# Three GINE layers of a graph network: gather indices kept on the chip, a ring of eight groups, sums kept in PSUM

## What is computed

```python
for l in range(3):
    e = edge_attr @ W_lin[l] + b_lin[l]                 # 32 -> 128 features
    msg = jax.nn.relu(x[src] + e)
    agg = jax.ops.segment_sum(msg, dst, num_segments=n)
    h = x + agg
    h = jax.nn.relu(h @ W1[l] + b1[l]) @ W2[l] + b2[l]
    x = jax.nn.relu(batchnorm(h, gamma[l], beta[l]))    # mean and variance over the nodes
```

## Time and profile before

| | us |
|---|---|
| median of three runs | 4933.01 |
| lowest and highest | 4932.24, 4936.58 |
| span of the profiled execution, first to last instruction | 5756.4 |
| TensorE busy in it, modelled | 4376.5 (76%) |
| VectorE busy | 2580.0 (45%) |
| GpSimd busy | 2560.5 (44%) |
| ScalarE busy | 1654.2 (29%) |
| mean granted clock of TensorE | 0.760 |

### The profile page before, as it was taken

The page is one execution under the profiler, slowest core; times in us unless marked ns, Lnnn a source line. Parts: engine busy times, 40 slices in busy tenths (PEclk is TensorE's granted clock), DMA queues, the critical chain, the costliest instruction groups (busy, mean ns, idle before and its releaser), DMA issues. The chain is left out here.

```text
span 5756.4 us, 93753 instructions
## 1 busy us (share of the span) xinstructions
PE 4376.5 (76%) x20714; PEld 3248.6 (56%) x20715; DVE 2580.0 (45%) x5638; ACT 1654.2 (29%) x3154; POOL 2560.5 (44%) x2647
## 2 busy tenths in 40 slices
PE   2799999566777547677477775677765999999995
PEld 2566666344444336666366664566653666666663
DVE  4677777644444432333222232233224445445444
ACT  1455555333343311111111111111112333333332
POOL 0455555255555335555255552555531333333330
PEclk9999999788888855555555555555557999999997
DMA  1333333122222111112121111121111222222220
GB/s 64 84 91 90 93 92 91 45 55 59 59 61 60 39 45 50 46 49 53 36 50 50 48 50 37 48 51 50 50 31 50 74 75 73 74 75 73 74 70 11
DMA packets 302152, 342.02 MB, mean 59 GB/s; under 512 B 154871, under 2 KB 227396, under 8 KB 301854
## 3 DMA queue, kind: packets, MB, share of 16 engines
q0 software_dynamic: 101632, 237.91, 15.2%
q1 hardware_dynamic: 182910, 79.61, 6.1%
q10 hardware_dynamic: 17568, 24.01, 1.5%
HBM read 324.54 MB, written 15.96 MB: 59 GB/s over the span
## 5 line engine op out<-in xcount | busy, mean ns | idle before, releaser
L777 POOL DMA_INDIRECT gath<-source_rows_narrow,idx x1176 | 1140.4, 970 | 1157.4 <-issue 865.6
L805 PE MATMUL psum<-hot,pm 128*128 128x128 f32 x2928 | 758.3, 441 | 601.6 <-ACT pm L860 566.6
L805 PEld LDWEIGHTS psum<-hot,pm 128*128 128x128 f32 x2928 | 651.4, 327 | 690.0 <-ACT pm L860 591.7
L903 POOL DMA_INDIRECT gath<-source_rows,idx x488 | 462.5, 948 | 879.5 <-issue 716.4
L795 PE MATMUL psum<-gine_lin,ea 32*128 32x128 f32 x2928 | 757.2, 436 | 56.0 <-DMA ea<-in_edge_attr 54.8
L860 ACT ACTIVATE pm<-vs 128x512 f32<-128x512 f32 x366 | 230.3, 629 | 1893.3 <-DVE vs L830 1609.5
L795 PEld LDWEIGHTS psum<-gine_lin,ea 32*128 32x128 f32 x2928 | 650.2, 323 | 141.0 <-DMA ea<-in_edge_attr 79.8
L556 POOL DMA_INDIRECT gath<-source_rows,idx x488 | 473.3, 970 | 556.3 <-PE psum L605 288.8
L556 POOL DMA_INDIRECT gath<-source_rows_narrow,idx x488 | 478.9, 981 | 440.1 <-PE psum L605 171.4
L830 DVE TENSOR_TENSOR vs<-psum,gath 128x512 f32<-128x512 f32 x366 | 253.2, 692 | 666.1 <-remote 292.0
L588 PE MATMUL psum<-lk,att_b 128*128 128x512 f32 x732 | 420.1, 663 | 131.5 <-DVE lk L678 87.9
(11 more groups left out here) (188 smaller groups left out, 5753.6 us busy)
## 6 DMA issues: line engine op xcount, KB each, us to landing
rel<-rel_rows SPq DMA_DIRECT2D x366, 128.0 KB
gath<-source_rows_narrow,idx POOLq DMA_INDIRECT x1664
ea<-in_edge_attr ACTq DMA_DIRECT2D x366, 64.0 KB
gath<-source_rows,idx POOLq DMA_INDIRECT x976
ea<-in_edge_attr SPq DMA_DIRECT2D x122, 64.0 KB
source_rows<-stage SPq DMA_DIRECT2D x12, 512.0 KB, 2.9
idx<-idx_all SPq DMA_DIRECT2D x366, 2.0 KB
source_rows_narrow<-TMP SPq DMA_DIRECT2D x3, 1600.0 KB, 7.3
```

The costliest lines, as they stand in the source:

```text
L777: pool.indirect_dma_start(out=gath[:, slot, j, 0:D], out_offset=None, in_=table1, in_offset=bass.IndirectOffsetOnAxis(ap=idx[:, slot, j:j ...
L805: last = e.matmul(O[s], pm[:, s, j * P:(j + 1) * P], hot[:, s, j, :], start=(j == 0), stop=(j == SUBS - 1))
L903: pool.indirect_dma_start(out=gath[:, s4, j, :], out_offset=None, in_=table, in_offset=bass.IndirectOffsetOnAxis(ap=idx[:, s4, j:j + 1], a ...
```

## The change

The indices of all groups are loaded once, in setup, into `idx_group`; the indirect DMAs read them from there and SP loads none in a layer. The ring has eight slots; `gath` is the same memory, cut into 8 x 4 x 128 in place of 4 x 4 x 256 of which half the width was used. SP only counts freed slots (`gi_free`). The edge features are loaded three items ahead, into four buffers. E has one bank, number 7, and TensorE waits for VectorE's add before it writes the next E. The sums of all blocks stay in banks 0 to 6: TensorE clears them by seven matmuls with zeros, then adds each item's four products at the block's place, whose number it reads into a register; VectorE has no add of the sums, and `gine_mlp` reads them from PSUM. The loops over layers, items and groups are written out.

```diff
+RING = 8
+        idx_group = sb("idx_group", [P, GROUPS, SUBS], I32)
...
+                        sp.dma_start(idx_group[:, :, :], t["src_by_group"]).then_inc(loads, 16)
...
-                        sp.wait_ge(loads, 7 * 16)
+                        sp.wait_ge(loads, 8 * 16)
...
-                        step(v.tensor_scalar(gb_i[:, 1:2], gb_i[:, 0:1], 3, None, ALU.bitwise_and))
+                        step(v.tensor_scalar(gb_i[:, 1:2], gb_i[:, 0:1], RING - 1, None, ALU.bitwise_and))
...
-            E = [psum[:, s, :] for s in range(2)]
-            O = [psum[:, 2 + s, 0:P] for s in range(2)]
+            ring = gath[:, :, :, :].rearrange("p s j d -> p (s j d)").rearrange("p (s j d) -> p s j d", s=RING, d=D)
+            ea_slots = [ea[:, 0, :], ea[:, 1, :], sm[0:EDGE_D, 0, :], sm[0:EDGE_D, 1, :]]
+            flat_psum = psum[:, :, :].rearrange("p a n -> p (a n)")
+            E = psum[:, 7, :]
+            zeros = hot_t[:, 0, :]
...
                 @block.sync
                 def _(sp):
-                    def group(g, slot, round):
-                        if not isinstance(g, int) or g >= 4:
-
-                            end = sp.value_load(group_end[0:1, bass.ds(g - 4, 1)], min_val=1, max_val=ITEMS)
-                            sp.wait_ge(gi["added"], done + end)
-                        sp.wait_ge(gi_gath[slot], 16 * SUBS * turn_of(slot, round))
-                        sp.dma_start(idx[:, slot, :], t["src_by_group"][bass.ds(g, 1), :, :].rearrange("a p j -> (a p) j")).then_inc(gi_idx[slot], 16)
-
-                    by_group(sp, group)
+                    for g in range(GROUPS - RING):
+                        end = sp.value_load(group_end[0:1, g:g + 1], min_val=1, max_val=ITEMS)
+                        sp.wait_ge(gi["added"], done + end)
+                        sp.nop().then_inc(gi_free, 1)
...
+                    pool.wait_ge(gine_stored, 16 * (layer + 1))
+                    for g in range(GROUPS):
+                        if g >= RING:
+                            pool.wait_ge(gi_free, layer * (GROUPS - RING) + g - RING + 1)
                         for j in range(SUBS):
                             pool.indirect_dma_start(
-                                out=gath[:, slot, j, 0:D], out_offset=None, in_=table1,
-                                in_offset=bass.IndirectOffsetOnAxis(ap=idx[:, slot, j:j + 1], axis=0)).then_inc(gi_gath[slot], 16)
+                                out=ring[:, g % RING, j, :], out_offset=None, in_=table1,
+                                in_offset=bass.IndirectOffsetOnAxis(ap=idx_group[:, g, j:j + 1], axis=0)).then_inc(gi_gath[g % RING], 16)
+                        if g > 0:
+                            landed(g - 1)
+                    landed(GROUPS - 1)
...
+                    e.wait_ge(gi["cleared"], layer + 1)
+                    for bank in range(7):
+                        e.matmul(psum[:, bank, :], zeros[:, 0:P], zeros, start=True, stop=True)
+
+                    def edges(i):
+                        e.wait_ge(gi_ea[i % 4], 16 * (layer * ea_uses(i % 4) + i // 4 + 1))
+                        e.wait_ge(gi["added"], done + i)
                         for j in range(SUBS):
-                            last = e.matmul(E[s][:, j * D:(j + 1) * D], ea[:, s, j * P:(j + 1) * P], gine_lin[:, :],
+                            last = e.matmul(E[:, j * D:(j + 1) * D], ea_slots[i % 4][:, j * P:(j + 1) * P], gine_lin[:, :],
                                             start=True, stop=True)
                         last.then_inc(gi["e_ready"], 1)
 
-                    def back(i, s, turn, s4, turn4):
-                        n = done + i
-                        e.wait_ge(gi["msg"], n + 1)
-                        e.wait_ge(gi["hot_done"], n + 1)
-                        e.wait_ge(gi["acc_done"], n)
+                    def sums(i):
+                        b = block_of(e, i)
+                        e.wait_ge(gi["hot_done"], done + i + 1)
+                        e.wait_ge(gi["msg"], done + i + 1)
                         for j in range(SUBS):
-                            last = e.matmul(O[s], pm[:, s, j * P:(j + 1) * P], hot[:, s, j, :], start=(j == 0), stop=(j == SUBS - 1))
+                            last = e.matmul(flat_psum[:, bass.ds(b * P, P)], pm[:, i % 2, j * P:(j + 1) * P], hot[:, i % 2, j, :],
+                                            start=False, stop=(j == SUBS - 1), skip_group_check=True)
                         last.then_inc(gi["o_ready"], 1)
 
-                    walk(e, front, back, layer=layer)
+                    edges(0)
+                    for i in range(1, ITEMS):
+                        edges(i)
+                        sums(i - 1)
+                    sums(ITEMS - 1)
...
-                    v.memset(acc, 0.0).then_inc(gi["cleared"], 1)
-                    v.wait_ge(gi["cleared"], layer + 1)
+                    v.memset(zeros, 0.0).then_inc(gi["cleared"], 1)
...
-                    def back(i, s, turn, s4, turn4):
-                        n = done + i
-                        b = block_of(v, i)
-                        v.wait_ge(gi["acc_done"], n + 1)
-                        v.wait_ge(gi["o_ready"], n + 1)
-                        a_b = acc[:, bass.ds(b * P, P)]
-                        v.tensor_tensor(a_b, a_b, O[s], ALU.add).then_inc(gi["acc_done"], 1)
...
+                    for i in range(3):
+                        load(i)
+                    for i in range(ITEMS):
+                        if i + 3 < ITEMS:
+                            load(i + 3)
...
-                    v.tensor_tensor(h, h, XT[:, :], ALU.add).then_inc(gine_h, 1)
+                    v.tensor_tensor(h, psum[:, :, :].rearrange("p a n -> p (a n)")[:, 0:NPAD], XT[:, :], ALU.add).then_inc(gine_h, 1)
...
-        with nc.Fori(0, GINE_LAYERS) as layer:
+        for layer in range(GINE_LAYERS):
```

More of the change, by code:

```diff
@@ L826, in front @@
                         v.wait_ge(gi_landed, layer * GROUPS + g + 1)
[L827 removed]
+                        if i >= 2:
                             v.wait_ge(gi["msg"], done + i - 1)
[L829 to L831 removed]
@@ L833, in back @@
[L833 to L841 removed]
+                        v.wait_ge(gi["e_ready"], done + i + 1)
@@ L843, in _, with load @@
+                        v.tensor_tensor(vs[:, i % 2, :].rearrange("p (j d) -> p j d", j=SUBS), E.rearrange("p (j d) -> p j d", j=SUBS),
+                                        ring[:, bass.ds(slot, 1), :, :].rearrange("p a j d -> p (a j) d"), ALU.add).then_inc(gi["added"], 1)
                 @block.scalar
                 def _(a):
-                    def load(i, s):
+                    def load(i):
                         g = group_of(a, i)
-                        if not isinstance(i, int) or i >= 2:
-                            a.wait_ge(gi["e_ready"], done + i - 1)
-                        a.dma_start(ea[:, s, :], t["edge_attr"][bass.ds(g, 1), :, :].rearrange("a k e -> (a k) e")).then_inc(gi_ea[s], 16)
@@ L851, in _ @@
-                    load(0, 0)
-                    def item(i, s, turn, s4, turn4):
-                        n = done + i
-                        if not (isinstance(i, int) and i == ITEMS - 1):
-                            load(i + 1, 1 - s)
-                        if not isinstance(i, int) or i >= 2:
-                            a.wait_ge(gi["o_ready"], n - 1)
-                        a.wait_ge(gi["added"], n + 1)
-                        a.activation(pm[:, s, :], vs[:, s, :], ACT.Relu).then_inc(gi["msg"], 1)
@@ L862, in _ @@
-                    in_order(a, item, layer)
+                        if i >= 4:
+                            a.wait_ge(gi["e_ready"], done + i - 3)
+                        a.dma_start(ea_slots[i % 4], t["edge_attr"][bass.ds(g, 1), :, :].rearrange("a k e -> (a k) e")).then_inc(gi_ea[i % 4], 16)
+                    for i in range(3):
+                        load(i)
+                    for i in range(ITEMS):
+                        if i + 3 < ITEMS:
+                            load(i + 3)
+                        if i >= 2:
+                            a.wait_ge(gi["o_ready"], done + i - 1)
+                        a.wait_ge(gi["added"], done + i + 1)
+                        a.activation(pm[:, i % 2, :], vs[:, i % 2, :], ACT.Relu).then_inc(gi["msg"], 1)
```

65 lines of the change are left out of this document (20 added, 45 removed).

## The result

| | median us | lowest to highest | runs |
|---|---|---|---|
| before | 4933.01 | 4924.77 to 4937.89 | 5 |
| after | 4953.47 | 4950.0 to 4956.78 | 5 |

The ratio is 1.0038, its 95% interval 1.0026 to 1.0049: the change makes the kernel slower by 20 us. I had forecast 4914 us, faster. The measured time is inside my range, on the side to which I had given 0.28.

The account below looks back on a forecast made before the run. GpSimd's gathers and TensorE's batches, both with floors near 495 us, plus hold-ups were taken to bound each edge pass. Timed: 4933 - 15 (resident indices) - 5 (layer turns) + 1 (setup) = 4914 us; range 4805 to 5000.

Parts of the forecast that it names:

- how much of that is in the timed runs: Edge passes: of the 823 us between profile and median, at least 443 lie there, leaving 0 to 37 us hold-ups, 18 taken.
- my floor of 509: One GINE edge pass without hold-ups: GpSimd and TensorE floors near 495 us, plus some 12 us at start and end.
- My bound of 56 us for the first attention pass: First attention pass: the profile could have added at most 904 - 848 = 56 us, as TensorE is busy for 848.
- no hold-ups in timed runs: Rival: GpSimd and TensorE each run through the timed edge passes, so no change, 4929 us; chance 0.22.
- Indices resident: Edge passes: a freed slot reaches GpSimd 1.9 us sooner per standstill; 162 us profiled, 5 us a pass or 15 timed.
- GpSimd's floor: Each edge pass: 392 gathers at 968 ns with 0.30 us between two make 497 us.
- The turn of a layer: Between layers: 0.7 us from index loads, 0.4 from loop branch and registers, 0.5 at pass end; 1.6 a layer, 5 us.
- The sums in PSUM: Edge passes: VectorE loses 121 adds and a register load, 35 us a pass and more, hidden behind TensorE; counts 0.
- One bank for E: TensorE's wait for L830 before the next E: covered by 1.1 us, cost 0; the block's register load also 0.
- slower: Rival: TensorE's loop gets longer through the one bank or block's register load, 0.2 us an item, 5002 us; chance 0.28.
- Loops written out: Instruction fetch: more than 18 packets to fetch; bounds 0 and +100 us, taken as 0.
- the ring of eight: Edge passes: GpSimd can be seven groups ahead, not three; cover for TensorE's hold-ups only, 0 to 37 us a pass, taken 0.

## Why the prediction was wrong

Two steps failed. One put a gain where there was none, 15 us; the other, GpSimd's time per gather taken as a constant, left out 26.5 us of loss, and that one turned the sign: without it the other terms, as measured, would have made after some 8 us faster. With the turns, which gave 5 us more than I had, and 1 us more over the rest, they make 37 of the 39 us between 4914 and 4953.

**The first step that failed is "how much of that is in the timed runs".** I split the 823 us between page and median by bounds and left 0 to 37 us of hold-ups in a pass, took 18, and gave it as the step that I trust least. What the runs showed: none. From its first gather to its last add a pass of before takes 506 to 508 us in the short condition, which is my floor of 509, and not 527. No add in the three passes comes more than 5.6 us after the one before it; in the page there are 28 to 30 steps a pass of over 7 us, 12.5 us on average. The 823 us lie 519 in the passes (173 of each one's 185), 180 in the second attention pass, 79 in the first, 40 in the turns. My bound of 56 us for the first attention pass was wrong, since TensorE's busy time is itself longer in the long condition (832.7 against 794.6 us); the bound of 241 for the second held. The rival "no hold-ups in timed runs", 4929 us, had the state of before right.

**Indices resident, -15 us.** It was to save 1.9 us at each standstill of GpSimd. In the short condition no gather of before starts more than 0.6 us behind the end of the last one, so there are none and the term is 0. The 1.9 us itself was about right, 2.59 to 0.78 us in the long condition; the 85 of the page were TensorE's waits, while GpSimd itself stood still there for over 0.6 us 130 times.

**The second step that failed is GpSimd's floor, which I took as the same after the change.** I took 968 ns a gather as a constant. It is 943 with a tail that VectorE makes: a mean of 972 before and 994 after, in the short condition. The number of gathers does not change, but the tail depends on where in GpSimd's 1.25 us the compare falls, thus on the order of work that the change rewrites. This term was missing: +26.5 us, in the gathers (33.5 to 60.0) as in the passes (1497.5 to 1523.9). I had read VectorE's spare time as free ("counts 0"); its instructions cost nothing in its own time, but one of them costs GpSimd's. The row that could have told it was there: a mean of 968 ns over gathers of which the rows show single ones at 0.95.

**The turn of a layer, -1.6 us each, 5 in all.** It gave 10.4 us in this profile of after (5.7, 5.7 and, in the last turn, 1.0 lost), 14.7 and 14.3 in the next two. The first turn splits so, after and then before with its layers written out:

```profile
2312.20 0.94 POOL L774 DMA_INDIRECT gath<-source_rows_narrow,idx_group  x1 [0.30 <-issue]
...
2320.63 3.49 DVE L1139 TENSOR_TENSOR ACC<-psum,XT 128x3200 f32<-128x3200 f32 x1 [3.35 <-PEq L755]
```

```profile
2305.27 0.94 POOL L777 DMA_INDIRECT gath<-source_rows_narrow,idx  x1 [0.30 <-issue]
...
2315.80 3.49 DVE L1155 TENSOR_TENSOR ACC<-ACC,XT 128x3200 f32<-128x3200 f32 x1 [2.73 <-PEq L740]
```

8.4 us from the last gather to the residual's add, where it was 10.5; the table's store to the first gather takes 7.57 us and not 9.83, as no index load stands before it (I had 0.7 of these 2.3). The rest, 1.3 us, is in the work between.

**Right.** The sums in PSUM freed 28 us of VectorE a pass and gave nothing. One bank for E and the block's register load on TensorE cost nothing that shows in three passes: with the compare in four those of after are 1474 us and those of before 1469, and the 5 us between them are what is left of the lengthening (9.9 against 5.2). TensorE's batches are 2.00 to 2.01 us apart there, and L791's waits for L827 fall from 75.7 to 32.2 us with no change to the bank, so more than half of them were the late gathers passed on. The rival "slower" blamed that bank and that register load: it had the sign by luck and the cause wrong. Loops written out: the instruction queue carries 71 packets and not 18, and in the stages that stayed the same nothing shows beyond some 2 us; the layer loop alone, written out, made 1.0003. The clock stayed at 0.50, with TensorE busy 482.6 of 508 us.

**In the long condition** the sum gave the change 166 us and it gained 71. Two terms were wrong: resident indices are worth 91 us and not 162, and the ring of eight, taken as 0, costs. With four slots the whole change takes 0.9726 of before, 159 us less, near my 166, but not by my terms, as the resident indices alone are 91 of it. With eight it is 0.9885. After's turns are 388 us there with eight slots and 321 with four: GpSimd runs up to eight groups ahead while TensorE is held up, and some 20 items are still to be added when the last gather has ended, with four slots 10 (the last add ends 39.8 and 19.1 us after that gather's start).

**Open.** Which part of the change moved the compare: in after it starts 0.1 us after TensorE begins the batch that follows the products into the sums, in before it stands behind L839, which the sums in PSUM removed; that is how the rows read, but the runs that undo this part all met the long condition. Resident indices alone raised the lengthening there too. Also open is what makes the long condition.

## What to carry to other kernels

Where a page is longer than the timed runs by more than its own scatter, first run the unchanged kernel again: a sum made against another condition repairs waits that the timed runs don't have. An engine with time to spare is not free of cost to others: look for the spread of an instruction that paces the loop (0.94 or 1.36 us for the same gather) and lay the other engines' instructions beside its long ones. Here one operand in PSUM takes the collision away (its worth in time was not measured in the short condition), and four short compares with one SBUF tensor each take most of it, worth 52 us on after and 26 on before.

## What the hardware showed that I had not expected

Two engines with loops of 1.25 and 4.01 us locked into step by the very delay that one gives the other: 137 of 366 compares start within 100 ns of the same phase, against 39 in before. And in the long condition TensorE's batches are signalled late while GpSimd gathers without pause. In after there, a batch starts at 2203.26 us and is modelled as done at 2205.34; the compare that waits for it starts at 2208.12, when the gathers have stopped at 2206.13. The clock in the passes (0.50) and the single gather (0.94 us) are as in the short condition. That the gathers hold the signal back is how the rows read; no run tests it:

```profile
2203.26 2.08 PE L800 MATMUL psum<-hot,pm 128*128 128x128 f32 x8
...
2205.19 0.94 POOL L774 DMA_INDIRECT gath<-source_rows_narrow,idx_group  x1 [0.30 <-issue]
2208.12 0.69 DVE L816 TENSOR_TENSOR hot<-consts,rel_all 128x512 f32<-128x512 f32 x1 [6.98 <-remote]
```

The last edge pass, in which TensorE is busy nearly throughout and GpSimd stands still for over 0.6 us 123 times, takes 1183 to 1185 us in both conditions.
